# Second graph aggregation: 44 of its 64 adjacency pieces as f16 high and low parts, three products each

## The chip, the cores and the metric

One core of one Trainium2 chip. The metric is the device time of one execution in microseconds (us). Engines are called by the profile's names: PE (TensorE; PEld is its weight load), DVE (VectorE), ACT (ScalarE), POOL (GpSimd), SP (SyncE, here a queue of DMAs).

## The reference

Four layers over 2048 rows x of 128 features, each with a residual, in fp32:

```python
x = x + gnn0(layernorm(x), adj, adj)   # tanh-filtered adjacency, top 350 a row
x = x + ffn0(layernorm(x))             # 8 experts of width 256, 2 chosen
x = x + gnn1(layernorm(x), adj, w)     # the layer of this change
x = x + ffn1(layernorm(x))             # 4-head causal attention, then 8 experts, 2 chosen

def gnn1(x, adj, w):
    A = adj + eye
    d_isqrt = rsqrt(sum(A, axis=1))
    h = (A * d_isqrt[:, None] * d_isqrt[None, :]) @ x
    return elu(h @ w)
```

## The kernel before

The transposed adjacency lies in SBUF as `A` (16 tiles j of 128 source rows by 2048 targets, fp32), loaded for the first layer. The rows of x are 16 tiles of 128, in NC = 4 chunks c of TPC = 4 tiles, so a chunk is 512 columns (CW). `G` holds the normalised rows times the degree factor `dis`, also fp32.

**The second aggregation** (`aggregate`, L1557): for chunk c, 16 products, one for each tile j, of `G[:, j]` (weights) with the 512 columns of `A[:, j]` that belong to c, summed in PSUM bank c % 2. A product of this size is called a piece; there are 64. The four tiles j of c's own chunk also get a product with the identity, for the eye. A piece in fp32 shows as two MATMUL records. PE's order is: c = 0, j 0 to 3; c = 1, j 0 to 3; c = 0, j 4 to 15; c = 1, j 4 to 15; then c = 2 and c = 3. Into this PE puts, at fixed places (c, j), the work on chunks already aggregated: `times_w(c-1)` at (1, 6), (2, 2), (3, 2); `transposed_rows(c-2)` at (2, 3), (3, 1); `query_products(c-2)` at (2, 7), (3, 4); `key_value_products(c-2)` at (2, 11), (3, 8), which waits for the rotated queries of its chunk (`s_qr`); and in c = 3 the 16 `max` units of attention's chunk 0 at j = 3, 5, 7, 9, 10, 11 and its `neg` unit at j = 13.

**Each engine works through its own list in order.** ACT in this stage: `aggregate_copy(0)` (L1207, PSUM to `hagg`), `elu_exp(0)`, `aggregate_copy(1)`, `high1(0)`, `elu_exp(1)`, then the high parts of queries and keys of chunk 0, `aggregate_copy(2)` and so on to `elu_exp(2)`, `aggregate_copy(3)`. DVE: rows of `G` (`rows_of_gnn1`, L2089), then the attention weights (L2144 to L2155, once their DMA is there), and at the end of its program text `elu_and_statistics(0)` (L2160 to L1924), `layer1_rows(0)` (L2189, with a `normalise`, L1929), `low1(0)`, `elu_and_statistics(1)`, `rotate` and `low_of_rotated` for queries (L2208 to L2218) and keys of chunk 0, `layer1_rows(1)`, `low1(1)`, the units of chunk 0 mixed with the rotation of chunk 1, `elu_and_statistics(2)`, `layer1_rows(2)`, and then the units of attention's steps, the first of which, `w` of chunk 3, reads PSUM at L2160 again. POOL: four inverse roots for the rows of `G` (L953, L954), small constants (L957 to L970), then `rows_root(0)`, `(1)`, `(2)` (L972: a power, L975, that waits for DVE's statistics of that chunk, and two memsets, L979). SP: after the low parts of queries and keys of a chunk it stacks them by DMA (`stack`, L731).

**The hand-over to attention** on PE: after the last piece it waits for `aggregate_copy(3)` (`s_hagg`), then makes the scores of the first step (L1745, L1747) and, at the start of that step, the `w` unit (L1699). The expert layer before the stage (L1489, L1506 on PE; L1155, L1157 on ACT; L2059 on DVE; L908 to L921 on POOL) already works with f16 high and low parts: L2059 is `scale x fp32 - high` into a f16 tile, L919 and L921 `fp32 - high` on POOL.

Of the kernel before, what the change touches and what calls it, by code (L numbers as in the profile page):

```python
# [6 lines left out]
F16 = mybir.dt.float16  # L7
BF16 = mybir.dt.bfloat16
I32 = mybir.dt.int32
ALU = mybir.AluOpType  # L10
# [48 lines left out]
SX = 32.0  # L59
SW = 256.0  # L60
# [33 lines left out]
def program(nc, x_in, adj_t, adj_in, w_proj, b_proj, w_gcn, b_gcn, f0_wg, f0_bg, f0_bias, f0_w1, f0_b1,  # L94
            f0_w2, f0_b2, g1_w, ln1, ln2, wq, wk, wv, wo, w_router, f1_w1, f1_w2, f1_w3, cos_t, sin_t, out):
    with ExitStack() as ctx:
# [35 lines left out]
        g_last = sb("g_last", [P, 3 * P], F16)  # L132
        st_b1 = sb("st_b1", [P, 2, K0])
# [46 lines left out]
        frow = R[:, 6 * CW:8 * CW].rearrange("p (b t) -> p b t", b=2)  # L180
        cos_sb = R[:, 2 * T:3 * T]
# [188 lines left out]
        s_acts = sem("scalar_steps")  # L370
# [39 lines left out]
        s_hhi = sem("hidden0_high")  # L410
# [460 lines left out]
        def _(pool):  # L871
# [64 lines left out]
            pool.tensor_tensor(dis[:, :], sm[:, 11, :], neg_half[:, :], ALU.pow).then_inc(s_dis, 1)  # L936
# [9 lines left out]
            chain(pool.tensor_copy(ident_b[:, :], ident[:, :]))  # L946
            pool.tensor_copy(ident_h[:, :], ident[:, :]).then_inc(s_mc, 1)
# [7 lines left out]


# [67 lines left out]

            for g in range(NC - 1):
                rows_root(g)
            chain(pool.tensor_scalar(factor[:, 3:4], cols[:, 3:4], SW, None, ALU.mult))
# [69 lines left out]
        def _(act):  # L1097
# [105 lines left out]
            def aggregate_copy(c):  # L1203
                act.wait_ge(s_agg1, c + 1)
                if c >= 2:
                    act.wait_ge(s_z, c - 1)
                act.activation(hagg[:, c % 2, :], ps[:, c % 2, :], ACT.Copy).then_inc(s_hagg, 1)  # L1207
# [26 lines left out]

            aggregate_copy(0)
            elu_exp(0)
            aggregate_copy(1)
            high1(0)
            elu_exp(1)
            high_queries(0)  # L1240
# [136 lines left out]
        def _(pe):  # L1377
# [179 lines left out]
            def aggregate(c, tiles):  # L1557
                if c >= 2:
                    pe.wait_ge(s_hagg, c - 1)
                for j in tiles:  # L1560
# [13 lines left out]
                    if j // TPC == c:  # L1574
                        q = j % TPC
                        pe.matmul(ps[:, c % 2, P * q:P * q + P], G[:, j, :], ident[:, :], start=(j == 0), stop=False,
                                  skip_group_check=True)
                    last = pe.matmul(ps[:, c % 2, :], G[:, j, :], A[:, j, CW * c:CW * c + CW],  # L1578
                                     start=(j == 0 and c > 0), stop=(j == NT - 1), skip_group_check=True)
# [327 lines left out]
        def _(dve):  # L1907
# [235 lines left out]

            dve.wait_ge(s_attw, AGAIN + 16 * (2 * 2 + 5))  # L2144
# [351 lines left out]

            elu_and_statistics(0)
            layer1_rows(0)
            low1(0)
            elu_and_statistics(1)  # L2500
            for what in (of_queries, of_keys):
# [145 lines left out]
```

## Time and profile before

| | us |
|---|---|
| median of 3 runs (lowest, highest) | 577.62 (574.78, 579.01) |
| span of the profiled execution | 610.4 |
| second aggregation in it, first product to last | 205.0 to 283.0 |

Times of rows are microseconds from the span's start. In a timeline or chain row the first number is the start, the second the length; `xN` is the number of merged instructions, and `[t <-X]` says that the engine was idle for t before it and that X ended that. Instructions of one engine overlap a little, so the distance of two starts is less than a length. The profiled execution is longer than the unprofiled runs; differences are worked out inside it.

### The profile page before, as it was taken

To read this page: it belongs to the slowest core of one execution; us is meant where nothing else is said; L and a number is where in the kernel's file an instruction comes from. 1 tells how busy PE (TensorE), PEld (TensorE's weight loads), DVE (VectorE), ACT (ScalarE), POOL (GpSimd) and SP (SyncE) were. 2 spreads that over 40 slices of the span, in tenths; PEclk is the share of its full clock that TensorE was granted. 3 is DMA by queue.
4 is the path that set the end of the run, shared out by engine and by line. 5 is a ranking of instruction groups with operands and counts; after the bars stand their busy time and mean duration, and the time that the engine had idled before them with its cause. 6 is when DMAs were issued, how large, how long until landed. Compare 5 with 4: busy or idle time off the path is not lost.

```text
span 610.4 us, 11302 instructions
## 1 busy us (share of the span) xinstructions
PE 501.5 (82%) x3819; PEld 281.4 (46%) x3819; DVE 429.3 (70%) x1065; ACT 314.3 (51%) x522; POOL 254.2 (42%) x275
## 2 busy tenths in 40 slices
PE   2999986699999799996776888998969657498880
PEld 1533334477777445443322432333412157397770
DVE  6898838888999925757786896999752038166564
ACT  0787985869999001201254453764745334166661
POOL 3000005133436401102364895997353632555562
PEclk9999995999999799999578789999989859599996
DMA  8999954100139250110233522003035447389925
GB/s 302 409 421 422 405 189 149 42 19 20 34 129 411 85 109 0 39 26 15 68 110 99 157 72 60 2 1 104 35 129 177 176 121 222 112 277 384 324 89 175
DMA packets 39570, 93.43 MB, mean 153 GB/s; under 512 B 7488, under 2 KB 24944, under 8 KB 35168
## 3 DMA queue, kind: packets, MB, share of 16 engines
q1 hardware_dynamic: 35072, 86.96, 40.6%
q0 software_dynamic: 2272, 4.69, 2.2%
q10 hardware_dynamic: 2176, 1.13, 0.6%
q8 instruction: 28, 0.46, 0.3%
q14 instruction: 22, 0.18, 0.1%
HBM read 69.39 MB, written 21.00 MB: 148 GB/s over the span
## 4 chain that ended last, share of the span: by engine, by line
PE 54%; DVE 21%; ACT 7%; issue 6%; another core or an unknown queue 5%; DMA 4%; POOL 1%; SPq 1%; DVEq 0%; POOLq 0%; ACTq 0%
PE ps L1578 8%; DVE A L2385 7%; PE ps L1755 6%; PE ps L1489 6%; PE ps L1506 6%; PE ps L1404 5%; PE ps L1859 3%; PE ps L1656 3%; PE ps L1747 3%; DMA R<-in_adj_in 3%; PE ps L1842 2%; PE ps L1603 2%; PE ps L1381 1%; DVE bst L1916 1%
## 5 line engine op out<-in xcount | busy, mean ns | idle before, releaser
L2385 DVE TENSOR_REDUCE A<-ps 128x1 f32<-128x512 f32 (+3 forms) x160 | 86.3, 601 | 13.7 <-PE ps L1656 13.0
L1302 ACT ACTIVATE A<-ps 128x1024 f32<-128x1024 f32 (+3 forms) x80 | 68.4, 894 | 49.2 <-PE ps L1747 40.3
L1007 POOL TENSOR_TENSOR G<-G,A 128x1024 f32<-128x1024 f32 (+3 forms) x40 | 73.8, 1888 | 9.1 <-ACT A L1302 8.9
L1656 PE MATMUL ps<-A 96*128 96x512 f16 (+3 forms) x160 | 55.4, 388 | 10.4 <-DVE A L2385 5.1
L1578 PE MATMUL ps<-A,G 128*128 128x512 f32 x128 | 62.1, 611 | 0.0
L1404 PE MATMUL ps<-R,G 128*128 128x512 f32 x128 | 59.2, 605 | 1.0 <-DVE G L1959 0.8
L1859 PE MATMUL ps<-A 128*128 128x128 f16 (+1 forms) x702 | 50.3, 228 | 6.0 <-issue 6.0
L1506 PE MATMUL ps<-R 128*128 128x128 f16 x768 | 48.2, 219 | 6.7 <-DVE x L2077 5.8
L1506 PEld LDWEIGHTS ps<-R 128*128 128x128 f16 x768 | 45.3, 98 | 14.3 <-issue 6.6
L1747 PE MATMUL ps<-A 97*128 97x512 f16 (+3 forms) x160 | 45.2, 366 | 6.9 <-ACT A L1302 5.1
L2059 DVE SCALAR_TENSOR_TENSOR R<-R 128x512 f16<-128x512 f32 x64 | 46.7, 754 | 5.0 <-ACT R L1157 4.7
L1859 PEld LDWEIGHTS ps<-A 128*128 128x128 f16 (+1 forms) x702 | 45.7, 107 | 8.0 <-issue 7.6
L1489 PE MATMUL ps<-G,R 128*128 128x512 f16 x192 | 48.3, 387 | 1.3 <-ACT R L1157 1.2
L1155 ACT ACTIVATE R<-ps,b 128x512 f32<-128x512 f32 x64 | 44.0, 688 | 10.2 <-PE ps L1489 9.3
L1052 POOL DMA_INDIRECT slots_in<-R,A x32 | 31.8, 993 | 39.5 <-ACT A L1302 13.8
L1157 ACT ACTIVATE R<-ps,b1s 128x512 f16<-128x512 f32 x64 | 44.2, 690 | 0.0
L1755 PE MATMUL ps<-A 128*32 128x512 f32 (+3 forms) x320 | 41.9, 599 | 0.0
L908 POOL TENSOR_TENSOR R<-R,factor 128x256 f32<-128x256 f32 (+1 forms) x28 | 18.3, 662 | 49.0 <-PE ps L1506 29.5
L1947 DVE SCALAR_TENSOR_TENSOR R<-A 128x2048 f32<-128x2048 f32 x16 | 36.5, 2284 | 0.9 <-issue 0.9
L2077 DVE SCALAR_TENSOR_TENSOR x<-ps,sm,x 128x128 f32<-128x128 f32 x128 | 35.8, 341 | 0.9 <-DVE sm L2067 0.8
L896 POOL TENSOR_TENSOR roots<-variances,neg_half 128x4 f32<-128x4 f32 x2 | 2.0, 1020 | 81.9 <-DVE variances L1924 81.9
L1404 PEld LDWEIGHTS ps<-R,G 128*128 128x128 f32 x128 | 23.0, 189 | 27.7 <-issue 25.9
(311 smaller groups left out, 933.0 us busy)
## 6 DMA issues: line engine op xcount, KB each, us to landing
A<-w_split SPq DMA_DIRECT2D x39, 533.0 KB
A<-in_adj_t SPq DMA_DIRECT2D x16, 1024.0 KB, 17.5
slots_in<-xn SPq DMA_DIRECT2D x1, 8320.0 KB, 22.4
R<-in_adj_in SPq DMA_DIRECT2D x7, 1024.0 KB, 6.1
w_split<-A SPq DMA_DIRECT2D x9, 725.0 KB, 4.1
xn<-in_adj_in SPq DMA_DIRECT2D x5, 1024.0 KB
xT<-in_adj_in SPq DMA_DIRECT2D x4, 1024.0 KB
A<-in_f_w SPq DMA_DIRECT2D x16, 170.5 KB
```

What stands on the lines that cost most here:

```text
L1007: pool.tensor_tensor(total, total, probabilities(n, pair)[:, :, t0:CW], ALU.add).then_inc(s_sum, 1)
L1302: act.activation(probabilities(n, pair)[:, :, t0:CW], ps[:, 2 * pair:2 * pair + 2, t0:CW], ACT.Exp, scale=1.0 / (SQ * SQ * float(HD) ** 0. ...
L1404: last = pe.matmul(ps[:, c, :], G[:, j, :], fbuf[:, j % FB, CW * c:CW * c + CW], start=(j == 0), stop=(j == NT - 1))
L1489: last = pe.matmul(ps[:, H_BANKS[u % 4], :], w[:, s, P * k:P * k + P], a[:, CW * g:CW * g + CW], start=(n == 0), stop=(n == 2))
L1506: last = pe.matmul(ps[:, 2 + gg % 2, P * q:P * q + P], a[:, gg % 4, k, P * q:P * q + P], w[:, s, k, :], start=(n == 0), stop=(n == 3 * K0 ...
L1578: last = pe.matmul(ps[:, c % 2, :], G[:, j, :], A[:, j, CW * c:CW * c + CW], start=(j == 0 and c > 0), stop=(j == NT - 1), skip_group_chec ...
L1656: last = pe.matmul(ps[:, bank, 0:width], queries(t // TPC, h)[0:KQ, P * (t % TPC):P * (t % TPC) + P], keys(b, h // (NH // NKV))[0:KQ, 0:wi ...
L1747: last = pe.matmul(ps[:, h, t0:CW], keys(j // TPC, h // (NH // NKV))[0:KQ + 1, P * (j % TPC):P * (j % TPC) + P], queries(c, h)[0:KQ + 1, t ...
L1755: last = pe.matmul(ps[HD * h:HD * h + HD, bank, t0:CW], weights(h), source(h // 2)[:, h % 2, t0:CW], start=start, stop=stop, skip_group_ch ...
L1859: last = pe.matmul(ps[0:w, bank + n % 2, P * k:P * k + P], first_weights[:, 2 * H1 * part + o:2 * H1 * part + o + w], a, start=i == 0, sto ...
L2059: dve.scalar_tensor_tensor(out=hh_lo[:, gg % 4, k, :], in0=h32[:, u % 4, :], scalar=SH, in1=hh_hi[:, gg % 4, k, :], op0=ALU.mult, op1=ALU. ...
L2385: dve.reduce_max(pm[:, h, t % TPC, b:b + 1], ps[:, bank, 0:width], AX_X).then_inc(s_rmf, 1)
```

## The change

The 20 pieces that come first (all of c = 0, and c = 1 with j 0 to 3) stay fp32. The other 44, numbered k = 0 to 43 in PE's order (c = 1 has 0 to 11, c = 2 has 12 to 27, c = 3 has 28 to 43), are split into two f16 parts: high = f16(1024 a), low = f16(1024 a - high). `G` is split in pairs of tiles, m = 0 to 7. PE then makes three f16 products for a piece (high x high, high x low, low x high), and two with a f16 identity instead of one in fp32.

High parts are ACT's (`high_piece`), 44 of them. The low part is DVE's for 27 pieces (`scalar_tensor_tensor`) and POOL's for the 17 in `by_pool`, for which ACT first also scales the fp32 piece in place. The 8 pairs of `G` are high on ACT, low on DVE. The first seven pieces have homes in `R`, which is free once the last expert output is there; every later piece k takes the place of the fp32 piece k - 7, so that its high part waits for that piece's low part. Pair m of `G` goes where pair m - 1 was, once its fp32 products are done (`s_g32`) and its low part is made.

The new work stands in each engine's list between the old: ACT does `HIGHS` up to piece 21 and g7 ahead of `aggregate_copy(0)`, the rest in blocks between the old steps; DVE does `LOWS` up to g7 ahead of the attention weights, five behind them, two behind `elu_and_statistics(0)`, two behind `layer1_rows(0)`, two behind `low1(0)`, five behind `elu_and_statistics(1)`; POOL does its 12 pieces of c = 1 and 2 ahead of the small constants, 30 and 33 behind `rows_root(0)`, 36 and 39 behind `rows_root(1)`, 42 behind `rows_root(2)`. The scale goes into `dis` (one more small operation on POOL) and is taken out in `aggregate_copy`.

```diff
 SX = 32.0
+SA = 1024.0
+SG = SA * SX
 SW = 256.0
...
+        g_first = sb("g_first", [P, 4 * P], F16)
+        ident_a = sb("ident_a", [P, P], F16)
...
+        pieces = [(c, j) for c in range(1, NC) for j in range(TPC if c == 1 else 0, NT)]
+        piece_no = {piece: k for k, piece in enumerate(pieces)}
+        HOMES1 = [v.bitcast(F16) for v in (zs[:, 0, :], ez[:, 0, :], frow[:, 0, :], hagg[:, 1, :], zs[:, 1, :], ez[:, 1, :], frow[:, 1, :])]
+        AHEAD = len(HOMES1)
+        by_pool = [k for k in range(len(pieces)) if (k % 2 == 0 if pieces[k][0] == 1 else k % 3 == 0)]
+        def piece(k):
+            c, j = pieces[k]
+            return A[:, j, CW * c:CW * c + CW]
+        def piece_halves(k):
+            home = HOMES1[k] if k < AHEAD else piece(k - AHEAD).bitcast(F16)
+            return home[:, 0:CW], home[:, CW:2 * CW]
+        def g_pair(m):
+            return G[:, 2 * m:2 * m + 2, :].rearrange("p t d -> p (t d)")
+        def g_halves(m):
+            home = g_pair(m - 1).bitcast(F16) if m else g_first[:, :]
+            return home[:, 0:2 * P], home[:, 2 * P:4 * P]
+        HIGHS = [*range(0, 7), "g0", 7, 8, 9, "g1", 10, 11, 12, "g2", 13, 14, "g3", 15, 16, "g4", 17, 18, "g5", 19, 20, "g6", 21, "g7",
+                 *range(22, len(pieces))]
+        LOWS = [1, 3, 5, "g0", 7, 9, "g1", 11, "g2", 13, "g3", 14, "g4", 16, "g5", 17, "g6", 19, "g7",
+                *[k for k in range(20, len(pieces)) if k % 3]]
+        high_no = {what: n for n, what in enumerate(HIGHS)}
+        low_no = {what: n for n, what in enumerate(LOWS)}
+        pool_no = {k: n for n, k in enumerate(by_pool)}
+        assert sorted([*by_pool, *[k for k in LOWS if isinstance(k, int)]]) == list(range(len(pieces)))
+        def wait_for_low(eng, k):
+            if k in pool_no:
+                eng.wait_ge(s_lowp, pool_no[k] + 1)
+            else:
+                eng.wait_ge(s_lowd, low_no[k] + 1)
...
-            pool.tensor_tensor(dis[:, :], sm[:, 11, :], neg_half[:, :], ALU.pow).then_inc(s_dis, 1)
+            chain(pool.tensor_tensor(dis[:, :], sm[:, 11, :], neg_half[:, :], ALU.pow))
+            pool.tensor_scalar(dis[:, :], dis[:, :], SG, None, ALU.mult).then_inc(s_dis, 1)
...
+            pool.tensor_scalar(ident_a[:, :], ident[:, :], SA, None, ALU.mult)
...
+            def low_piece(k):
+                pool.wait_ge(s_high, high_no[k] + 1)
+                high, low = piece_halves(k)
+                pool.tensor_tensor(low, piece(k), high, ALU.subtract).then_inc(s_lowp, 1)
+            for k in by_pool:
+                if pieces[k][0] < NC - 1:
+                    low_piece(k)
...
+            late_pieces = [k for k in by_pool if pieces[k][0] == NC - 1]
             for g in range(NC - 1):
                 rows_root(g)
+                for k in late_pieces[2 * g:2 * g + 2] if g < NC - 2 else late_pieces[2 * g:]:
+                    low_piece(k)
...
-                act.activation(hagg[:, c % 2, :], ps[:, c % 2, :], ACT.Copy).then_inc(s_hagg, 1)
+                act.activation(hagg[:, c % 2, :], ps[:, c % 2, :], ACT.Copy, scale=1.0 / (SG * SG)).then_inc(s_hagg, 1)
...
+            def high_piece(k):
+                if k >= AHEAD:
+                    wait_for_low(act, k - AHEAD)
+                high, _ = piece_halves(k)
+                last = act.activation(high, piece(k), ACT.Copy, scale=SA)
+                if k in pool_no:
+                    last = act.activation(piece(k), piece(k), ACT.Copy, scale=SA)
+                last.then_inc(s_high, 1)
+            def high_g(m):
+                act.wait_ge(s_xn, 2 * NC - ON_SCALAR + (2 * m + 1) // TPC + 1)
+                if m:
+                    act.wait_ge(s_g32, m)
+                    act.wait_ge(s_lowd, low_no[f"g{m - 1}"] + 1)
+                act.activation(g_halves(m)[0], g_pair(m), ACT.Copy, scale=1.0 / SA).then_inc(s_high, 1)
+            def highs(a, b):
+                for what in HIGHS[a:b]:
+                    if isinstance(what, int):
+                        high_piece(what)
+                    else:
+                        high_g(int(what[1:]))
+            in_order = lambda k: high_no[k]
+            act.wait_ge(s_y0, E0 * NC + 4)
+            highs(0, in_order(22))
             aggregate_copy(0)
+            highs(in_order(22), in_order(30))
             elu_exp(0)
+            highs(in_order(30), in_order(32))
             aggregate_copy(1)
+            highs(in_order(32), in_order(37))
             high1(0)
+            highs(in_order(37), in_order(40))
             elu_exp(1)
+            highs(in_order(40), len(HIGHS))
             high_queries(0)
             values_and_high_keys(0)
             aggregate_copy(2)
...
-                    if j // TPC == c:
-                        q = j % TPC
-                        pe.matmul(ps[:, c % 2, P * q:P * q + P], G[:, j, :], ident[:, :], start=(j == 0), stop=False,
-                                  skip_group_check=True)
-                    last = pe.matmul(ps[:, c % 2, :], G[:, j, :], A[:, j, CW * c:CW * c + CW],
-                                     start=(j == 0 and c > 0), stop=(j == NT - 1), skip_group_check=True)
+                    q = j % TPC
+                    if (c, j) in piece_no:
+                        k = piece_no[c, j]
+                        wait_for_low(pe, k)
+                        if c == 1:
+                            pe.wait_ge(s_lowd, low_no[f"g{j // 2}"] + 1)
+                        (g_high, g_low), (high, low) = g_halves(j // 2), piece_halves(k)
+                        own = slice(P * (j % 2), P * (j % 2) + P)
+                        for n, (g, a) in enumerate(((g_high, high), (g_high, low), (g_low, high))):
+                            last = pe.matmul(ps[:, c % 2, :], g[:, own], a, start=(j == 0 and n == 0),
+                                             stop=(j == NT - 1 and n == 2), skip_group_check=True)
+                        if j // TPC == c:
+                            for g in (g_high, g_low):
+                                last = pe.matmul(ps[:, c % 2, P * q:P * q + P], g[:, own], ident_a[:, :], start=False, stop=False,
+                                                 skip_group_check=True)
+                        if k < AHEAD:
+                            last.then_inc(s_used, 1)
+                    else:
+                        if j // TPC == c:
+                            pe.matmul(ps[:, c % 2, P * q:P * q + P], G[:, j, :], ident[:, :], start=(j == 0), stop=False,
+                                      skip_group_check=True)
+                        last = pe.matmul(ps[:, c % 2, :], G[:, j, :], A[:, j, CW * c:CW * c + CW],
+                                         start=(j == 0 and c > 0), stop=(j == NT - 1), skip_group_check=True)
+                        if j % 2 and (c == 1 or j >= TPC) and not (c == 0 and j == NT - 1):
+                            last.then_inc(s_g32, 1)
                 if tiles[-1] == NT - 1:
                     last.then_inc(s_agg1, 1)
...
+            def low_piece(k):
+                dve.wait_ge(s_high, high_no[k] + 1)
+                high, low = piece_halves(k)
+                dve.scalar_tensor_tensor(out=low, in0=piece(k), scalar=SA, in1=high, op0=ALU.mult, op1=ALU.subtract).then_inc(s_lowd, 1)
+            def low_g(m):
+                dve.wait_ge(s_high, high_no[f"g{m}"] + 1)
+                high, low = g_halves(m)
+                dve.scalar_tensor_tensor(out=low, in0=g_pair(m), scalar=1.0 / SA, in1=high, op0=ALU.mult, op1=ALU.subtract).then_inc(s_lowd, 1)
+            def lows(a, b):
+                for what in LOWS[a:b]:
+                    if isinstance(what, int):
+                        low_piece(what)
+                    else:
+                        low_g(int(what[1:]))
+            before = lambda k: low_no[k]
+            lows(0, before(20))
             dve.wait_ge(s_attw, AGAIN + 16 * (2 * 2 + 5))
             for src, ln, a, b in ((wq32, 2, WQ, WQR), (wk32, 2, WK, WKR), (wv32, 2, WV, WR), (wr32, 3, WR, WR + 8)):
                 chain(dve.tensor_scalar(src, src, cols[:, ln:ln + 1], SW, ALU.mult, ALU.mult))
...
+            lows(before(20), before(28))
+            dve.wait_ge(s_used, 2)
             elu_and_statistics(0)
+            lows(before(28), before(31))
+            dve.wait_ge(s_used, 3)
             layer1_rows(0)
+            lows(before(31), before(34))
             low1(0)
+            lows(before(34), before(37))
             elu_and_statistics(1)
+            lows(before(37), len(LOWS))
             for what in (of_queries, of_keys):
                 rotate(0, *what)
                 low_of_rotated(0, *what)
```

## Rows read from the trace of the kernel before

**Rows 1.** The page, part 1: busy time, share of the span and instructions.

```profile
PE 501.5 (82%) x3819; PEld 281.4 (46%) x3819; DVE 429.3 (70%) x1065; ACT 314.3 (51%) x522; POOL 254.2 (42%) x275
```

**Rows 2.** Busy time of PE, PEld, DVE, ACT, POOL, PE's clock, DMA by stretch.

```profile
211.40:225.90 14.50, 14.50 (x36) 6.44 (x35) 4.01 (x17) 0.00 (x0) 2.91 (x13) 1.00 0.71 152
225.90:247.90 22.00, 22.00 (x78) 11.61 (x77) 12.78 (x54) 3.05 (x5) 2.77 (x3) 1.00 0.00 0
...
264.60:280.40 15.80, 14.17 (x67) 6.29 (x66) 11.56 (x22) 1.64 (x3) 0.00 (x0) 1.00 0.16 37
```

**Rows 3.** The chain that ended last, 204 to 292 (start, length).

```profile
211.54 14.59 PE ps L1578 x34
...
226.13 0.22 PE ps L1576 x2
...
245.56 1.29 PE ps L1603 x6
...
280.43 1.14 DVE R L2160 x4
...
285.21 1.65 POOL roots L975
```

**Rows 4.** Timeline of PE ahead of the stage.

```profile
202.59 1.58 PE L1506 MATMUL ps<-R 128*128 128x128 f16 x24 [2.27 <-DVE x L2077]
```

**Rows 5.** Timeline of ACT, copies from SBUF.

```profile
249.98 0.63 ACT L1220 ACTIVATE A<-A 128x512 f16<-128x512 f32 x1 [4.34 <-DVE A L2212]
...
317.11 0.51 ACT L1283 ACTIVATE A<-A 128x384 f16<-128x384 f32 x1
317.52 0.85 ACT L1284 ACTIVATE A<-A,factor 128x682 f32<-128x682 f32 x1
```

**Rows 6.** Timeline of DVE.

```profile
143.07 2.07 DVE L2059 SCALAR_TENSOR_TENSOR R<-R 128x512 f16<-128x512 f32 x2
...
200.11 1.29 DVE L2059 SCALAR_TENSOR_TENSOR R<-R 128x512 f16<-128x512 f32 x2
...
223.43 0.28 DVE L2146 TENSOR_SCALAR R<-R,cols 128x128 f32<-128x128 f32 x1 [9.77 <-DMA R<-in_w_router]
...
229.22 1.12 DVE L2160 TENSOR_SCALAR R<-ps,dis 128x128 f32<-128x128 f32 x4 [1.91 <-PE ps L1588]
...
235.62 1.30 DVE L2189 TENSOR_SCALAR R<-x,mv,roots 128x128 f32<-128x128 f32 x4 [1.76 <-POOL roots L975]
...
243.40 1.12 DVE L2160 TENSOR_SCALAR R<-ps,dis 128x128 f32<-128x128 f32 x4
...
247.94 1.28 DVE L2208 SCALAR_TENSOR_TENSOR A<-ps,R 128x512 f32<-128x512 f32 x2
...
289.13 1.11 DVE L2160 TENSOR_SCALAR R<-ps,dis 128x128 f32<-128x128 f32 x4
```

**Rows 7.** Timeline of POOL.

```profile
142.27 0.67 POOL L919 TENSOR_TENSOR R<-R 128x256 f16<-128x256 f32 x1
...
143.59 1.00 POOL L921 TENSOR_TENSOR R<-R 128x256 f16<-128x256 f32 x1
...
212.31 0.20 POOL L954 TENSOR_TENSOR roots<-roots,dis 128x4 f32<-128x4 f32 x1
...
286.91 1.13 POOL L979 MEMSET A<- 1x512 f16 x2
...
420.94 0.90 POOL L988 TENSOR_TENSOR A<-A 128x384 f16<-128x384 f32 x1
```

**Rows 8.** Timeline of PE at the hand-over; last row by stretch, columns of rows 2.

```profile
283.81 0.23 PE L1745 MATMUL ps<-R 128*128 128x128 bf16 x1 [0.69 <-ACT R L1207]
...
285.04 1.05 PE L1699 MATMUL ps<-wmat,R 128*128 128x128 f32 x8
...
290.30 0.61 PE L1656 MATMUL ps<-A 96*128 96x512 f16 x1 [3.87 <-DVE R L2160]
...
290.30:302.70 12.40, 10.32 (x53) 4.86 (x54) 8.30 (x17) 2.09 (x4) 4.41 (x5) 0.50 0.26 77
```

More of the change, by code:

```diff
@@ L369, in program @@
         s_dve = sem("vector_steps")
-        s_acts = sem("scalar_steps")
+        s_high = sem("adj_piece_high_ready")
+        s_lowd = sem("adj_piece_low_by_vector")
+        s_lowp = sem("adj_piece_low_by_gpsimd")
+        s_used = sem("adj_piece_multiplied")
+        s_g32 = sem("gnn1_row_pair_multiplied")
         s_var = sem("variance_ready")
@@ L409, in program @@
         s_relu = sem("hidden0_relu")
-        s_hhi = sem("hidden0_high")
         s_hlo = sem("hidden0_low")
```

## The prediction

> **What bounds it now.** I read the page first: TensorE (PE) is the busiest engine, VectorE (DVE) the next, ACT and POOL far behind [rows 1]. The change touches only the second aggregation, so I cut that stage into stretches: PE is busy for all of 211.4 to 247.9 and for 14.2 of the 15.8 us up to 280.4, at the full granted clock, while ACT is nearly idle, POOL as well, and DVE is busy for 12.8 of 22.0 and 11.6 of 15.8 us [rows 2]. The chain that ended last runs through PE until 280.4 and then leaves it: `elu_and_statistics(2)` on DVE, the root on POOL, `layer1_rows(2)`, the read of the bank of the `w` unit (L2160), the first reductions [rows 3]. So PE paces the stage, DVE has slack, but what hands over to attention is DVE's order, and it is DVE, ACT and POOL that get the new work.
>
> **What PE gains.** Seventeen fp32 pieces take 14.59 us, 0.858 each [rows 3]; six f16 products of the same width take 1.29, 0.215 each [rows 3]. Three of them are 0.645, so 44 pieces save 9.4 us. Twelve identity products of 0.22 [rows 3] become two f16 ones of about 0.055, saving 1.3. Together 10.7 us, if nothing waits.
>
> **What the others pay.** ACT: 44 high parts, 17 scaled copies, 8 of G. A 512-wide one lasts 0.63, which bounds its pitch from above; two of 384 elements start 0.41 apart, so I take 0.41 x 512/384 = 0.55, and for the 256-wide ones 0.33, between 0.27 by the same ratio and 0.41 [rows 5]: 61 x 0.55 + 8 x 0.33 = 36 us. DVE: 27 lows at 0.61 (two in 1.29) and 8 half as wide at some 0.4: 20 us [rows 6]. POOL: 17 lows; 384 elements of the same form take 0.90, so 512 take 1.2, less about 0.1 of overlap, 1.1: 19 us [rows 7]. Busy time would fit into the idle time; the order decides. The extra `dis` scaling and `ident_a` lie in POOL's idle time before the first root, `g_first` costs nothing, the longer semaphore lists neither.
>
> **Step 1, the first wave.** ACT starts when the last expert output is there, 204.2 [rows 4]. Pieces 0 to 6 (7 highs, 4 copies) and g0 end at 210.6. High 7 writes over piece 0 and waits for its low part, which POOL can't start before its last root is done, 212.5 [rows 7]: with 1.1 and a hop 213.7. From there 15 highs, 6 copies and 7 parts of G: 21 x 0.55 + 7 x 0.33 = 13.9, so g7 is ready at 227.6 and low g7 at 228.0. DVE is free from 213.7 [rows 6], keeps up with its 19 lows and waits with g7. `aggregate_copy(0)`, released by the 17 pieces' end at 226.1 before [rows 3], stands behind g7: 1.5 us later, felt by PE in `times_w(0)`, but not what decides.
>
> **Step 2, attention weights.** They stand behind `lows(0, before(20))`. Before, they waited for their DMA until 223.43 and ended 1.91 ahead of the first ELU, at 227.3 [rows 6], in time that DVE had idle; now 228.0 + 3.9 = 231.9. Five lows follow (3.05): `elu_and_statistics(0)` starts at 235.0, not 229.22 [rows 6], +5.8.
>
> **Step 3, a ring of waits.** ELU and statistics take 4.65 (229.22 to 235.62 less the 1.76 of waiting behind them [rows 6]), to 239.65. Two lows hide in the wait for the root (1.76 [rows 6]), rows and normalise 2.3, to 243.7; two lows, `low1`, two lows: 246.7 for `elu_and_statistics(1)`, not 243.40 [rows 6], +3.3; its variance is there at 251.3. Then five lows, the last for piece 43. Its high part goes over piece 36, so it waits for low 36, which POOL has only behind `rows_root(1)`: root 1.65 [rows 3], memsets 1.13 [rows 7], low 36 1.1, high 43 0.65, low 43 0.65, with hops to 256.7. Four lows (2.4) hide in it. `rotate(0, queries)` therefore starts at 256.7, not 247.94 [rows 6], +8.8. Behind it wait PE's `key_value_products(0)`, at (2, 11), and SP's stacks of chunk 0. PE, whose c = 2 pieces are quicker, stands there some 8 us.
>
> **Step 4, some comes back.** From there to `elu_and_statistics(2)` were 32.5 us. PE has 18 quicker pieces in it (3.9 us), but DVE is busy 11.6 of its last 15.8 us [rows 2] and waits for ACT in turn; I take 3.0 back (0 to 4). So E, its start, is at +5.8: 286.2.
>
> **Step 5, piece 42.** POOL's last low part stands behind `rows_root(2)`, and that behind the statistics of chunk 2, which DVE starts only after the `neg` unit that PE issues at (3, 13). PE then needs low 42 at (3, 14). Before, POOL's root started 4.8 after E, and the memsets were done at E + 7.6 [rows 3, 7]. So low 42 comes at E + 8.8, pieces 42 and 43 with identities (1.5) end at E + 10.3, the copy (0.65) at E + 11.0, and scores and `w` take as before 283.81 to 286.1 [rows 8]: E + 13.3. DVE wanted that bank at 289.1 [rows 6], E + 8.7; PE's slack, 3.87 us of idleness there [rows 8], is used up and 4.6 us more. Join: 5.8 + 4.6 = +10.4.
>
> **Step 6, DVE beside POOL.** All this took durations of engines left alone. A pair of L2059, the form of the new lows, took 1.29 alone and 2.07 beside POOL's L921, which itself took 1.00 where L919 took 0.67 [rows 6, 7]: 2.07 is nearly 1.29 + 0.67, as if one had waited for the other. Nothing at one end (all 17 lows of POOL fall into gaps). At the other, full exclusion: the first wave then holds 8 to 9 POOL lows and 19 DVE lows one after another, 9.4 + 9.9 = 19.3 from 213.7, 233 rather than 228, +5; and the other 8 POOL lows up to 0.6 each on DVE's path, +5: +10. I take the middle, +5, since POOL itself often waits for ACT in the wave.
>
> The Trainium skill ("SBUF — State Buffer", Who interferes with whom) says that a DVE instruction with two SBUF inputs and a GpSimd instruction that reads SBUF exclude each other, whichever started first. By that rule the sum ends at +20 rather than +15; the pair above agrees with it in its one instance.
>
> **Sum.** Join +10.4 + 5 = +15.4. What follows hangs on that join, so I pass it on whole: 610.4 + 15.4 = 625.8 for a profiled execution like this one. The span shown is 33 us above the median of the runs (577.62), but this stage ran at full clock in it, so I carry the difference over: 577.6 + 15.4 = 593.0.
>
> **Rivals.**
> (a) *Full exclusion of DVE and POOL*, +20.4: 598. For it the pair in [rows 6]; against it only how far the lows truly meet.
> (b) *The clock.* After 3.87 us of idleness PE had a granted clock of 0.50 for 12 us [rows 8]. The new stops (8 us at `key_value_products(0)`, 8 at piece 42) are longer. At half clock the six pieces left before `transposed_rows(1)` cost 3.9 us more and w, scores and pieces 42 and 43 up to 3, against DVE waits which cover part: 0 to +5 on top, up to 603.
> (c) *PE paces the stage to its end*, the other side: the lows lie in DVE's idle time and the 10.7 us come out less 1.5 for the copy: 568.4. For it, the idle shares [rows 2]. Against it two places of the order. Its test is the start R of `rotate(0, queries)`: the join moves by (R - 247.9) - 3.0 + 4.6, so it is faster only if R is before 246.3, and the lows and weights alone make that impossible unless ACT's and DVE's new work is half as long as their rows say.
> (d) *Taken back later.* Attention waits often for ACT and DMA, and a later start could close some of its gaps: 5 to 10 us less, 583 to 588, at most within 1%.
> (e) *The f16 products bring nothing*, since weight loads show: six in a row on other weights ran at 0.215 [rows 4], so hardly.
>
> **How the numbers follow.** Forecast with its own spread, 588 to 596: 0.52. (a) or (b) or both, 596 to 606: 0.27, 0.05 of it above 603. (d) 0.16, half of it still over 583.4 (more than 1% slower), half within 1%. (c) 0.05, (e) is inside the slower ones. A measurement of this kernel tells some 1% from no change. So faster 0.05, same 0.08, slower 0.87, and 584 to 603 leaves out 0.05 + 0.08 + 0.05 = 0.18.
>
> **What would show it.** In the changed profile: f16 pieces of about 0.65 us in c = 1; g7's high part near 227.6 and the first ELU near 235 or later (steps 1, 2); DVE waiting for the high part of 43 and PE several us for the query rotation (step 3); PE some 8 us before piece 42, released by POOL (step 5); mean DVE lows near 0.68 if step 6 is nothing, over 1 if (a). I am wrong if the query rotation starts before 250, if piece 42 is not waited for, or if the stages behind the join get shorter by more than 3 us.

## The result and the profile after

The changed kernel takes 599.85 us (median of 4 runs, 596.29 to 602.69), the kernel before, run beside it, 577.10 (574.78 to 579.01): a ratio of 1.0401 with an interval of [1.0363, 1.0439]. It is slower by 22.75 us. The forecast was 593.0 within 584 to 603, slower with a chance of 0.87. So the side was right and the range held, but the time lies above the forecast's own spread (588 to 596), where rivals (a) and (b) had put it; why is taken apart below.

A warning on the two profiled executions: that of before has a span of 610.4 us and that of after 598.7. The extra time of before lies late, behind the stage of this change (290.3 to its end takes 320.1 us, 311.9 to the end of after 286.8), and none of its runs without a profile shows it. I therefore compare the stage by itself, in both traces from the same event: S, the end of the last 24 products of the experts, 204.17 before [rows 4] and 205.97 after.

First the page, part 1, of the kernel after: busy time, share, instructions.

```profile
PE 481.9 (80%) x3863; PEld 272.8 (46%) x3863; DVE 461.1 (77%) x1100; ACT 349.7 (58%) x591; POOL 275.0 (46%) x294
```

Beside [rows 1]: PE lost 19.6 us of work, DVE gained 31.8, ACT 35.4, POOL 20.8. PE's difference is more than the forecast gain of 10.7, since the two executions differ elsewhere too; the stage has to be read in the timelines. By stretch (columns of [rows 2]), the first wave up to the query rotation, from there to `elu_and_statistics(2)`, and the hand-over:

```profile
205.97:268.00 62.03, 42.98 (x170) 21.10 (x169) 54.98 (x142) 38.09 (x74) 32.23 (x39) 0.86 0.18 38
266.80:296.90 30.10, 24.58 (x138) 11.80 (x138) 20.78 (x45) 4.37 (x8) 0.00 (x0) 0.92 0.17 40
296.90:312.00 15.10, 5.54 (x36) 3.14 (x33) 7.66 (x26) 1.89 (x4) 7.05 (x10) 0.77 0.10 29
```

PE was busy throughout the second aggregation before [rows 2]; now it works 43 of the first 62 us and DVE 55. The bound has moved from PE to DVE and to what DVE waits for. Now the timeline of DVE after (start, length, engine, line, operation, tiles, count, idle time before it and who ended it):

```profile
212.91 1.11 DVE L2200 TENSOR_SCALAR G<-x,mv,roots 128x128 f32<-128x128 f32 x4
214.43 4.49 DVE L2200 TENSOR_SCALAR G<-x,mv,roots 128x128 f32<-128x128 f32 x4 [0.40 <-POOL roots L1000]
...
233.80 1.17 DVE L2265 SCALAR_TENSOR_TENSOR G<-G 128x256 f16<-128x256 f32 x1 [0.32 <-ACT G L1310]
...
242.48 1.12 DVE L2292 TENSOR_SCALAR R<-ps,dis 128x128 f32<-128x128 f32 x4
...
265.95 0.96 DVE L2259 SCALAR_TENSOR_TENSOR A<-A 128x512 f16<-128x512 f32 x1 [2.66 <-ACT A L1299]
266.83 1.28 DVE L2340 SCALAR_TENSOR_TENSOR A<-ps,R 128x512 f32<-128x512 f32 x2
...
296.86 1.13 DVE L2292 TENSOR_SCALAR R<-ps,dis 128x128 f32<-128x128 f32 x4 [0.16 <-DVE R L2526]
...
311.88 1.12 DVE L2292 TENSOR_SCALAR R<-ps,dis 128x128 f32<-128x128 f32 x4 [5.39 <-PE ps L1810]
```

and of POOL and ACT after, at the same places:

```profile
214.34 4.49 POOL L1007 TENSOR_TENSOR R<-A,R 128x512 f16<-128x512 f32 x4
...
264.10 2.26 POOL L1007 TENSOR_TENSOR A<-A 128x512 f16<-128x512 f32 x2
...
304.49 1.15 POOL L1007 TENSOR_TENSOR A<-A 128x512 f16<-128x512 f32 x1
```

```profile
215.53 0.63 ACT L1299 ACTIVATE A<-A 128x512 f16<-128x512 f32 x1 [3.39 <-POOL R L1007]
...
265.29 0.63 ACT L1299 ACTIVATE A<-A 128x512 f16<-128x512 f32 x1 [4.71 <-POOL A L1007]
```

and of PE after:

```profile
204.47 1.50 PE L1598 MATMUL ps<-R 128*128 128x128 f16 x24 [2.27 <-DVE x L2188]
...
234.30 2.07 PE L1699 MATMUL ps<-wmat,R 128*128 128x128 f32 x8 [6.06 <-ACT R L1266]
...
240.27 3.40 PE L1675 MATMUL ps<-A,G 128*128 128x512 f16 x15
...
268.89 2.77 PE L1714 MATMUL ps<-xT,R 128*64 128x512 f16 x6 [8.57 <-DVE A L2344]
...
305.69 1.46 PE L1675 MATMUL ps<-A,G 128*128 128x512 f16 x3 [8.62 <-POOL A L1007]
307.16 1.49 PE L1675 MATMUL ps<-A,G 128*128 128x512 f16 x3
```

Read from S, four points of DVE's order make the comparison, for these two and for every kernel below: the first `elu_and_statistics` (ELU), the rotation of the queries of chunk 0 (R), `elu_and_statistics(2)` (E) and the read of the `w` bank, the join (J).

| kernel | ELU | R | E | J | J against before | time against before |
|---|---|---|---|---|---|---|
| before | 25.05 | 43.77 | 76.26 | 84.96 | | |
| after | 36.51 | 60.86 | 90.89 | 105.91 | +20.95 | +22.75 |
| piece 42 early | 36.51 | 60.88 | 90.90 | 99.54 | +14.58 | +16.8 |
| ring open | 36.51 | 58.72 | 88.75 | 97.39 | +12.43 | +13.1 |
| POOL reads nothing | 30.85 | 53.31 | 83.33 | 99.67 | +14.71 | +17.3 |
| rows first | 36.40 | 60.77 | 90.79 | 105.82 | +20.86 | +21.5 |
| both, ring open and no reads | 30.86 | 50.61 | 80.63 | 90.09 | +5.13 | +6.9 |
| f16 products alone | 24.24 | 39.98 | 68.72 | 77.43 | -7.53 | -6.6 |
| one column group | 24.18 | 40.48 | 72.98 | 81.68 | -3.28 | -2.4 |
| two column groups | 24.67 | 40.98 | 71.85 | 80.69 | -4.27 | -2.9 |
| one group, POOL shares | 24.54 | 40.57 | 73.06 | 81.77 | -3.19 | -2.8 |

The times follow the join, with 0.4 to 2.6 us on top in every row. In the pair of before and after, 1.80 us of it is S itself, which lies later in the trace of after. Where it comes from isn't known; the kernel with the f16 products alone, which splits nothing, has 0.9 of it too, so the splitting can't be all of it.

### The profile page after: what moved, and what is told of

Same layout as the page of the kernel before. It is cut to its first block, busy times and chain, and to the rows that moved or that the text cites. A ratio compares the mean times of both kernels' runs of the same rounds, so it can differ in the third digit from the quotient of the medians.

```text
span 598.7 us, 11537 instructions
## 1 busy us (share of the span) xinstructions
PE 481.9 (80%) x3863; PEld 272.8 (46%) x3863; DVE 461.1 (77%) x1100; ACT 349.7 (58%) x591; POOL 275.0 (46%) x294
## 4 chain that ended last, share of the span: by engine, by line
PE 47%; DVE 26%; DMA 10%; ACT 6%; issue 5%; POOL 3%; SPq 1%; POOLq 0%; DVEq 0%; ACTq 0%
DVE A L2517 8%; PE ps L1866 7%; PE ps L1581 6%; PE ps L1598 6%; PE ps L1496 5%; DMA R<-in_adj_in 5%; PE ps L1970 4%; PE ps L1858 3%; DMA A<-w_split 3%; PE ps L1767 3%; PE ps L1714 2%; DVE bst L2027 2%; DVE A L2259 2%; PE ps L1996 1%; PE ps L1675 1%
## 5 line engine op out<-in xcount | busy, mean ns | idle before, releaser
L1767 PE MATMUL ps<-A 96*128 96x512 f16 (+3 forms) x160 | 53.7, 373 | 7.5 <-DVE A L2517 4.2
L1970 PE MATMUL ps<-A 128*128 128x128 f16 (+1 forms) x702 | 47.6, 224 | 4.6 <-DMA A<-w_split 4.5
L1214 ACT ACTIVATE R<-ps,b 128x512 f32<-128x512 f32 x64 | 44.1, 689 | 10.4 <-PE ps L1581 9.4
L1970 PEld LDWEIGHTS ps<-A 128*128 128x128 f16 (+1 forms) x702 | 44.4, 105 | 6.5 <-DMA A<-w_split 5.8
L1111 POOL DMA_INDIRECT slots_in<-R,A x32 | 31.8, 992 | 29.6 <-DVE A L2425 12.8
L1866 PE MATMUL ps<-A 128*32 128x512 f32 (+3 forms) x320 | 38.5, 554 | 0.0
L1675 PE MATMUL ps<-A,G 128*128 128x512 f16 x99 | 28.0, 420 | 8.6 <-POOL A L1007 8.6
```

The source lines that it names most:

```text
L1767: last = pe.matmul(ps[:, bank, 0:width], queries(t // TPC, h)[0:KQ, P * (t % TPC):P * (t % TPC) + P], keys(b, h // (NH // NKV))[0:KQ, 0:wi ...
L1866: last = pe.matmul(ps[HD * h:HD * h + HD, bank, t0:CW], weights(h), source(h // 2)[:, h % 2, t0:CW], start=start, stop=stop, skip_group_ch ...
L1970: last = pe.matmul(ps[0:w, bank + n % 2, P * k:P * k + P], first_weights[:, 2 * H1 * part + o:2 * H1 * part + o + w], a, start=i == 0, sto ...
```

## Experiments

**1 and 2: the order of POOL's late low parts.** In the kernel after two of five stand behind `rows_root(0)`, two behind `rows_root(1)`, one behind `rows_root(2)`. Experiment 1 (piece 42 early) moves the last; experiment 2 (ring open) has `(late_pieces[0:4], late_pieces[4:], ())` in the same line.

```
             for g in range(NC - 1):
                 rows_root(g)
-                for k in late_pieces[2 * g:2 * g + 2] if g < NC - 2 else late_pieces[2 * g:]:
+                for k in (late_pieces[0:2], late_pieces[2:], ())[g]:
```

> The changed kernel, but POOL makes the low part of piece 42 behind rows_root(1), ahead of rows_root(2). My theory (step 5: PE waits for it at the hand-over, and DVE for PE) expects the 8.6 us stop of PE and DVE's 5.39 us stop ahead of the first unit of attention to go, and with it 5 to 6.5 us: 593.5 to 595. The rival, that the hand-over is paced by DVE anyway, expects 599 to 600.

Measured 594.02 us, ratio 1.0307 [1.0264, 1.0350]: 5.8 less. From E to J it is 8.64 us and not 15.02, what the kernel before needed (8.70), and DVE no longer waits at J. So the place of POOL's last low is the whole of the loss in the hand-over. PE's granted clock is part of that loss: it is 1.00 from E to J here and 0.77 in the kernel after.

> As the run before it, and POOL also makes pieces 36 and 39 ahead of rows_root(1). My theory (step 3: low 36 behind rows_root(1) holds high 43, low 43 and the rotation of the queries) expects DVE's 2.66 us wait for high 43 to go and the rotation to start 2.5 to 3 us earlier: 590.5 to 592. If the rest of DVE's order is what holds the rotation, it stays within 1 us of the run before it.

Measured 590.35 us, ratio 1.0228 [1.0183, 1.0273]: 9.5 less, 0.15 below the band. The stop of DVE for the high part of piece 43 is gone; its five lows run through. But R is only 2.16 us earlier than in experiment 1, not the 2.5 to 3 expected, because the two lows that POOL now makes sooner meet other work of DVE: the rows of `xn` (the `normalise` in `layer1_rows(0)`) take 3.73 us beside three lows, where they took 2.88 beside two in the kernel after and 1.09 in the kernel before. DVE's timeline:

```profile
250.42 3.73 DVE L2040 TENSOR_SCALAR xn<-x,mv,roots 128x128 f32<-128x128 f32 x4
...
261.62 3.10 DVE L2259 SCALAR_TENSOR_TENSOR A<-A 128x512 f16<-128x512 f32 x5
264.64 1.28 DVE L2340 SCALAR_TENSOR_TENSOR A<-ps,R 128x512 f32<-128x512 f32 x2
...
294.67 1.13 DVE L2292 TENSOR_SCALAR R<-ps,dis 128x128 f32<-128x128 f32 x4 [0.16 <-DVE R L2526]
...
303.31 1.11 DVE L2292 TENSOR_SCALAR R<-ps,dis 128x128 f32<-128x128 f32 x4
```

and POOL's:

```profile
250.43 3.39 POOL L1007 TENSOR_TENSOR A<-A 128x512 f16<-128x512 f32 x3
```

R, E and J are each 2.15 us earlier than with piece 42 alone. So opening the ring of step 3 brings 2.15 at the join, net of that meeting, and the order behind `rows_root(2)` costs 6.37.

**3: POOL does its share, but reads nothing.**

```
                 high, low = piece_halves(k)
-                pool.tensor_tensor(low, piece(k), high, ALU.subtract).then_inc(s_lowp, 1)
+                chain(pool.memset(low, 0.0))
+                pool.memset(low, 0.0).then_inc(s_lowp, 1)
```

> The changed kernel, but POOL fills the low parts of its 17 pieces with zeros (two writes of 512 elements, about 1.05 us as its subtraction alone) and reads nothing; these low parts are left out of the sum. If DVE and POOL exclude each other where both read SBUF (step 6), the first wave ends 4 to 7 us earlier, the lows of DVE have 0.68 each, and the whole is 6 to 9 us less: 591 to 594. If the wave is held by ACT's pace and the order alone, under 2 us less: 598 to 600.

Measured 594.56 us, ratio 1.0294 [1.0217, 1.0371]: 5.3 less, 0.6 short of the band for the time. The first wave did end as early as expected, ELU is at S + 30.85 in place of 36.51. POOL is as long busy (two writes of 0.54 in place of one subtraction of 1.15 to 1.28), and all that follows in DVE's order moves forward. These are groups of instructions on DVE and POOL, 204 to 312 (line, operation, tiles, shapes, count, busy time and mean ns of one, idle time before). The kernel after:

```profile
L2259 DVE SCALAR_TENSOR_TENSOR A<-A 128x512 f16<-128x512 f32 x24 | 17.7, 773 | 2.7 <-ACT A L1299 2.7
L2200 DVE TENSOR_SCALAR G<-x,mv,roots 128x128 f32<-128x128 f32 x16 | 7.8, 550 | 0.4 <-POOL roots L1000 0.4
L2265 DVE SCALAR_TENSOR_TENSOR G<-G 128x256 f16<-128x256 f32 x7 | 5.6, 806 | 1.8 <-ACT G L1310 1.8
...
L1007 POOL TENSOR_TENSOR A<-A 128x512 f16<-128x512 f32 x13 | 16.6, 1282 | 14.1 <-ACT A L1301 13.8
```

The kernel whose POOL reads nothing:

```profile
L2260 DVE SCALAR_TENSOR_TENSOR A<-A 128x512 f16<-128x512 f32 x24 | 15.5, 685 | 3.3 <-ACT A L1300 3.2
L2201 DVE TENSOR_SCALAR G<-x,mv,roots 128x128 f32<-128x128 f32 x16 | 4.5, 376 | 0.4 <-POOL roots L1000 0.4
L2266 DVE SCALAR_TENSOR_TENSOR G<-G 128x256 f16<-128x256 f32 x7 | 3.0, 425 | 3.1 <-ACT G L1311 3.0
```

The same instructions take 31.1 us beside POOL's subtractions and 23.0 without them: 8.1 us of DVE's time is waiting for POOL, booked as busy. The rows of `xn` are not among them; they add 2.3 (twelve in 6.0 and 3.7 us). R and E are 7.55 us earlier, J only 6.24, since DVE waited there 7.42 us for PE in place of 5.39. The trace shows where PE lost them: piece 42 starts at E + 8.83 in both kernels, but here the granted clock stayed at 0.50 from 299.5 to 306.5, over the `w` unit too:

```profile
305.10 1.91 PE L1811 MATMUL ps<-wmat,R 128*128 128x128 f32 x8
```

In the kernel after this unit took 1.05. The hold-up is not spread evenly. Of the 8.1 us, the 24 wide lows, of which I had thought, lose 2.2; the rows of G 3.3, nearly all of it in the last four; the seven lows of G 2.6. Those four, with 4.49 us in place of 1.11, are the clearest instance: they stand still while POOL makes its first four lows, 214.34 to 218.83.

The writes that stand in for the subtractions are not wholly free for DVE. Its lows keep their length beside them (685 ns), but a short `tensor_scalar` that takes 0.20 us at 232.23 takes 0.56 beside a write of 0.52, as these rows of DVE and POOL show:

```profile
233.01 0.56 DVE L2078 TENSOR_SCALAR R<-R 128x64 f16<-128x64 f32 x1
```

```profile
233.00 0.52 POOL L1007 MEMSET A<- 128x512 f16 x1 [1.75 <-ACT A L1302]
```

So the 7.55 us are a lower bound for what POOL's low parts cost DVE.

**4: the rows of G first.** POOL's first lows wait until all rows of G are there.

```
+            pool.wait_ge(s_xn, 2 * NC - ON_SCALAR + NC)
             for k in by_pool:
```

> The changed kernel, but POOL starts its low parts only when the last rows of G are there. If the four operations of L2200 lost 3.4 us to POOL's four lows (4.49 rather than 1.12 us), they take 1.12 again, POOL starts 1.2 us later, low 1 and high 8 come 3 us earlier, and 2 to 3 us are gained: 597 to 598. If they are slow for another reason, it costs the 1.2 us: 601.

Measured 598.74 us, ratio 1.0386 [1.0343, 1.0429], and ELU at S + 36.40, 0.1 earlier: a miss (597 to 598 was expected). The rows take 1.11 again, which shows that POOL's lows had held them, but now POOL is the one held up, by DVE's lows:

```profile
215.88 1.11 DVE L2201 TENSOR_SCALAR G<-x,mv,roots 128x128 f32<-128x128 f32 x4 [0.41 <-POOL roots L1000]
```

```profile
217.08 7.32 POOL L1007 TENSOR_TENSOR R<-A,R 128x512 f16<-128x512 f32 x4 [1.23 <-DVE G L2201]
```

Four lows of POOL in 7.32 us and not 4.49. Here moving one such instruction in time did not remove the conflict: both engines have work to the end of the wave, and the one handed it to the other. I had reckoned the 3.4 us of the rows as a loss that can be avoided by itself, and it was not.

**5: the f16 products without the splits.** On the kernel before, with one fixed pair of tiles:

```
+            pool.tensor_copy(fixed_a[:, :], A[:, 0, CW:2 * CW])
+            pool.tensor_copy(fixed_g[:, :], A[:, 1, CW:CW + P])
...
+                    if c > 1 or (c == 1 and j >= TPC):
+                        for n in range(3):
+                            last = pe.matmul(ps[:, c % 2, :], fixed_g[:, :], fixed_a[:, :], start=(j == 0 and n == 0),
+                                             stop=(j == NT - 1 and n == 2), skip_group_check=True)
...
```

> The kernel before, with the 44 fp32 pieces (and their identities) replaced by three f16 products each of one fixed pair of f16 tiles (two for an identity); no splits are made, so the sums of those 44 pieces are left out of the result, and all other work stays. This measures what the f16 products alone give. My theory (products are cheap, 0.645 us a piece in place of 0.85, but the rows of VectorE pace the last part of the stage) expects: 12 pieces of the second column group 2.5 us earlier, VectorE's chain from there on unchanged, w(0) 5 to 7 us earlier than in the kernel before, total 570.5 to 572.5. The rival that TensorE paces the whole stage expects all of 44 x 0.2 us and the identities: 9 to 10.7 us, total 566.5 to 568.5. The rival that f16 gives nothing expects 577.

Measured 570.00 us, ratio 0.9894 [0.9869, 0.9920], J 7.53 us earlier than before. That is between my estimate for the join (5 to 7) and PE's whole gain (10.7), nearer to mine, and 0.5 below my band for the time. PE's new stops show where the other 3 us stay, at DVE (the second and third row; the first, six products behind R, is for the clock, below):

```profile
247.56 1.48 PE L1616 MATMUL ps<-xT,R 128*64 128x512 f16 x6 [0.71 <-DVE A L2225]
...
261.95 0.23 PE L1667 MATMUL ps<-R 128*128 128x128 bf16 x1 [1.46 <-DVE A L2398]
...
269.34 0.23 PE L1667 MATMUL ps<-R 128*128 128x128 bf16 x1 [0.71 <-DVE A L2398]
```

With the order of the other work as it is, this is the most that the idea could bring if the parts came for nothing: 7.5 us. The change paid 28.5 us at the join for them.

**6: only the pieces of one column group.** Twelve pieces (c = 1, j = 4 to 15), all their low parts and six lows of G on DVE ahead of the attention weights, the halves of G in `xT`, which is free at that time.

```
-        pieces = [(c, j) for c in range(1, NC) for j in range(TPC if c == 1 else 0, NT)]
+        pieces = [(1, j) for j in range(TPC, NT)]
...
-        by_pool = [k for k in range(len(pieces)) if (k % 2 == 0 if pieces[k][0] == 1 else k % 3 == 0)]
+        by_pool = []
...
-            home = g_pair(m - 1).bitcast(F16) if m else g_first[:, :]
+            home = xT[:, 256 * (m - 2):256 * (m - 1)].bitcast(F16)
```

> The kernel after with only the 12 pieces of the second column group (row tiles 4 to 15) as f16 parts; the pieces of the third and fourth group stay fp32 products as before. GpSimd makes no low parts; the scaled copies fall away; VectorE makes the 12 lows and 6 lows of G ahead of the attention weights, the halves of G lie in a tile that is free then. My theory (the splits cost where VectorE has work of its own, the first of them lie in its idle time beside the first column group) expects 2 to 4 us less than before: 573.5 to 575.5. The rival that the f16 products or the first wave of splits themselves are the loss expects 578 to 583.

Measured 574.28 us (10 runs), ratio 0.9959 [0.9939, 0.9979], as expected: 2.35 us faster than the kernel before, and nothing of the computation is left out. DVE had waited 9.77 us for a DMA there [rows 6]; this wait now holds the 18 lows, and DVE still comes to ELU ahead of PE:

```profile
223.77 0.28 DVE L2260 TENSOR_SCALAR R<-R,cols 128x128 f32<-128x128 f32 x1 [0.45 <-DMA R<-in_w_router]
...
228.96 1.12 DVE L2274 TENSOR_SCALAR R<-ps,dis 128x128 f32<-128x128 f32 x4 [1.30 <-PE ps L1682]
```

**7: eight pieces of the next group too**, their lows in DVE's three stops of 1.3, 1.8 and 2.4 us.

```
+        pieces = [(1, j) for j in range(TPC, NT)] + [(2, j) for j in range(8, NT)]
...
+            lows(low_no[12], low_no[14])
             dve.wait_ge(s_used, 2)
             elu_and_statistics(0)
+            lows(low_no[14], low_no[17])
             dve.wait_ge(s_used, 3)
             layer1_rows(0)
+            lows(low_no[17], len(LOWS))
             low1(0)
```

> The kernel that splits only the 12 pieces of the second column group, with 8 pieces of the third group (row tiles 8 to 15) split as well; their highs on ScalarE in its idle time, their lows on VectorE in the three stops of 1.3, 1.8 and 2.4 us that it had in that stretch, no lows on GpSimd. TensorE needs 8 x 0.215 for the pieces and 4 x 0.11 us for the identities less, 2.2 us. My theory (a split is free only in VectorE's idle time, and these 8 x 0.62 = 5.0 us just fit in 5.6 us) expects 0.4 to 2.0 us less than the version with one group, 572.3 to 574. The rival that the lows come late for TensorE or push the rows of VectorE expects no gain or up to 2 us more, 574.3 to 576.

Measured 574.37 us, ratio 0.9961 [0.9934, 0.9988]: a miss, the gain over one group that I expected (0.4 to 2.0 us) isn't in the time, which lies where the rival had it. J is 0.99 us earlier than with one group, so half of PE's 2.2 us arrives there; a microsecond is within the two intervals, and whether the time gained it is left open.

**8: POOL shares the one group**, every other one of the 12 lows.

```
-        by_pool = []
+        by_pool = [0, 2, 4, 6, 8, 10]
```

> The version that splits only the 12 pieces of the second column group, with every other low part of these 12 (6 of them) on GpSimd in place of VectorE, and ScalarE's six scaled copies that this needs: the sharing of the kernel after in the first wave, and nothing else of it. If the two engines worked side by side, VectorE would be relieved of 6 x 0.62 = 3.7 us and the time would be the same or lower, 573 to 574.5. The theory of exclusion expects VectorE to be held up by the 6 x 1.12 us = 6.7 us of GpSimd, the last four rows of G at 4 us or more in place of 1.1, VectorE's first rows of the second aggregation 1 to 3 us later after its 1.3 us of slack is gone, 575 to 577.5.

Measured 574.47 us, ratio 0.9952 [0.9930, 0.9975]: the time that I had named for engines that work side by side (573 to 574.5), and not that of exclusion (575 to 577.5). The time alone would have decided wrongly, for in the trace the exclusion is there, the same row again:

```profile
214.25 4.49 DVE L2183 TENSOR_SCALAR G<-x,mv,roots 128x128 f32<-128x128 f32 x4 [0.40 <-POOL roots L997]
```

From this row to the end of the attention weights DVE took 16.3 us, with POOL keeping the lows of six pieces, and 14.7 in the kernel with one group, doing all twelve itself. So POOL's 6.8 us of work relieved DVE of 3.7 (an estimate, six lows at 0.62) and held it up by 5.3, the rest of the difference; the rows longer than their like in the kernel with one group, four rows of G and three lows of G, make 5.0 of it. Of the 1.6 us more, 1.3 were DVE's slack ahead of ELU, where it then waited no more. Help from POOL was worth less than nothing to DVE and cost nothing that the time shows, because there was slack left. What failed in my forecast was that step: I took the hold-up to be larger than the slack by 1 to 3 us, and it was larger by 0.3 to 0.4 (ELU at S + 24.54, and 24.18 with one group).

**9: experiments 2 and 3 together.**

> The kernel after with both changes at once: GpSimd's 17 low parts replaced by writes of zero that read nothing (the low parts of those 17 pieces are left out of the result), and these writes put ahead of the roots that they stood behind, four behind the first root and two behind the second. Apart, the two gave 5.3 and 9.5 us. If they are separate causes, together they give about 14 to 15 us: 584 to 587, and the rest of the loss, 7 to 10 us over the kernel before, is VectorE's own share of the split (27 lows, 8 lows of G) and ScalarE's order. If they overlap (an exclusion that is only felt because the ring is tight), expect 588 to 590.

Measured 584.20 us, ratio 1.0110 [1.0076, 1.0143], as expected for separate causes: 15.65 us less than the kernel after, where 9.5 + 5.3 make 14.8 (at J: 15.82, and 8.52 + 6.24 = 14.76).

## Why the prediction was right, and what was mis-sized

The account of the join, in us against the kernel before: the products bring -7.53 (experiment 5); the reads of POOL's subtractions and the places of its last lows cost 15.82 (experiment 9); the other 12.7 are what remains there: -7.53 + 15.82 + 12.66 = +20.95. Only the first two are shown by an experiment each; the third is what is left, and that it is DVE's own lows, ACT's order and the clock is argued from the rows.

In the terms of the prediction the same +20.95 are the order of the work (10.4 forecast), step 6 (5 forecast) and the clock (nothing in the sum). Measured were 7.55 for step 6, at R in experiment 3, and 3.0 for the clock, see below; that leaves 10.4 for the order. That this meets the forecast so closely is in part luck: without POOL's reads R was 9.54 later than before, forecast 8.8, and without the clock's loss R to E took 28.74, forecast 29.5; the two errors cancel.

*What PE gains*: 0.645 for a piece as forecast (15 products in 3.40, of which the last ends later than the pitch of 0.215). Rival (e) is out. That the gain does not pass through whole was right (step 4: rotation to E took 30.03 against the forecast 29.5).

*Step 1* named the wave's end with g7 at 228.0; it was 234.97, of which 1.8 is S. The wave was longer by 5.2 us, through what step 6 describes. *Step 2*: weights and five lows put ELU 7.0 behind that end in the forecast, 7.5 in the trace. Both chains are as told. One reading of mine was off without harm: in [rows 5] a copy of 384 elements is followed by one of 682, not by another of 384. The pitch of 0.55 taken from it was 0.52. And the 0.215 that rival (e) quotes stands in [rows 3], not in [rows 4], whose products are 128 wide.

*Step 3*: DVE waits for ACT's high part, that for POOL's low, that for the root, in this order (265.95, 265.29, 264.10 above), and PE stands 8.57 us for the rotated keys' input, forecast some 8. *Step 5*: POOL's last low ends at E + 8.78, forecast E + 8.8; PE waits 8.62 us. Experiments 1 and 2 move both places. The first gives back what the order says; the second gives back 3.0 us at the ring and loses 0.9 ahead of it, where POOL's lows now meet the rows of `xn`. The way from ELU to R was 2.6 us longer than forecast (24.35 against 21.7), 1.8 of it the rows of `xn` with 2.88 in place of 1.09: step 6 again.

*Step 6* was the mis-sized term. I took 5 from a range of 0 to 10; experiment 3 shows 7.55 at R and E, and 6.24 at J, where the clock took some back. Rival (a), full exclusion at +20.4, came nearest to the join's +20.95, but with 10 for what was 7.55 and nothing for the clock. The sign that I had named, the mean of DVE's lows (0.68 if step 6 is nothing, over 1 if (a)), would have misled: it was 0.77. The error was one of method: I weighed how often two *lows* would meet and took the middle. But POOL's subtractions also stop DVE's other instructions from SBUF, the rows of G foremost and those of `xn` next, which I had not counted at all, and the lows of G take 0.81 for 0.43. And ACT waits for whoever is late: its highs over pieces 0 and 1 waited 3.39 us each for a POOL and for a DVE low. The Trainium skill ("SBUF — State Buffer", Who interferes with whom) has the exclusion as a rule. The Trainium skill says in the same section that a `tensor_scalar` can take part in it as well, in a mode in which it uses both port pairs. The measurements agree with both as far as they go: the lows read two tiles of SBUF, the rows of G only one, and both are held up; in which mode the rows of G ran, no row shows. I had read the rule for the lows alone.

*The clock* was nothing in the sum and 0 to +5 as rival (b). At three places PE came out of idleness of 6.06, 8.57 and 8.62 us, and its granted clock behind them was 0.57 (234.30 to 238.00), 0.50 (268.89 to 271.60) and 0.55 (305.69 to 309.50), so mostly the lower of its two levels, 1.2 GHz. The work there ran at half rate: `times_w(0)` 2.07 us where eight such products took 1.05 [rows 8], six f16 products 2.77 us, over twice their pitch, pieces 42 and 43 1.46 and 1.49 us where three products else show 0.81.

Two of the places lie on the path. The last: E to J took 15.02, forecast 13.3, +1.7, and the two pieces are 1.3 of it. The second: behind R, the same six products took 1.48 us with a granted clock of 1.00 in experiment 5, where PE had been idle for only 0.71 us before them, and 2.77 here; that is 1.29 us, and R to E is shorter there by just as much, 28.74 against 30.03. So the clock cost 3.0 us of the join. At the first place DVE waits for PE nowhere from g7 to R in the trace of after, so nothing shows that it delays R; no experiment separates it. The forecast was thus short of the join by 8.3 at R (5 taken), 0.5 up to E and 1.7 behind it: 5.5 of the 20.95. The rest of the 6.85 us between 593.0 and 599.85, 1.3, lies outside the stage.

Rival (d), a loss that attention gives back, did not happen in any of the kernels: the times follow J. Rival (c) needed R before 246.3 on the clock of before, S + 42.1; it was S + 60.86. With the products alone it is S + 39.98, and that kernel is faster, as its condition says.

## What to carry to other kernels

Making the busiest engine's work cheaper pays only what the engines that prepare the operands can do in time in which they wait. The whole set of 44 pieces cost 28.5 us of preparation for a gain of 7.5, while the 12 pieces whose splits fitted into one DMA wait of VectorE brought 2.35 us net. Count a GpSimd subtraction between SBUF tiles as time of VectorE too where the two meet: in experiment 8 six of them held VectorE up by 5.3 us for 3.7 of relief. And look, for each operand made on a slow engine's queue, at what already stands ahead of it there: the place of a single low part of 1.15 us behind a root cost 5.8 us, and was had back by moving one entry of a list.

## What the runs showed of the hardware that I had not expected

VectorE's `tensor_scalar` with one tile of SBUF as input and another as output stood still for GpSimd's `tensor_tensor`: four in 4.49 or 4.50 us and not 1.11, in four kernels (after, experiments 1, 2 and 8), and 1.11 to 1.21 where GpSimd wrote only or waited. Writes of constants alone can hold a `tensor_scalar` up as well: 0.56 us for 0.20 beside one write in experiment 3, and in experiment 9 the four rows of `xn` below, 2.63 for 1.11 beside writes of 128x1024. The lows, a `scalar_tensor_tensor`, kept their 685 ns beside writes.

```profile
296.36 2.63 DVE L2041 TENSOR_SCALAR xn<-x,mv,roots 128x128 f32<-128x128 f32 x4
```

The hold-up is mutual: GpSimd's four lows took 7.32 us in place of 4.49 when VectorE's lows ran first. In a profile it hides in the busy time: neither engine shows a wait, only a mean duration (550 ns for 376, 806 for 425) that differs from the same instruction elsewhere.
